# GpSimd folds the sums over the embedding axis a second time: quarters on top of halves, before VectorE's reduction

## The reference

```python
e = jnp.stack([tbl_0[ids[:, 0]], tbl_1[ids[:, 1]],
...
tbl_31[ids[:, 31]]], axis=1)          # (1024, 32, 16)
x0 = e
xk = x0
outs = []
for W in (W0, W1, W2):                # (32, 32, 64), (32, 64, 64), (32, 64, 64)
    xk = jax.nn.relu(jnp.einsum('bmd,bhd,mhk->bkd', x0, xk, W))
    outs.append(jnp.sum(xk, axis=2))  # the sums over d
h = jnp.concatenate([jnp.concatenate(outs, axis=1), dense_ctx], axis=1)
h = jnp.maximum(h @ W_top1 + b_top1, 0.0)
h = jnp.maximum(h @ W_top2 + b_top2, 0.0)
y = h @ W_top3
```

## Time and profile before

| what | value |
|---|---|
| median of 3 runs | 665.38 us (665.16 to 666.02) |
| the profiled execution's own time | 664.73 us |
| its span, first to last instruction | 662.1 us |
| outside the span | 2.63 us |
| mean granted TensorE clock | 0.982 |
| busy: PE, DVE, ACT, POOL | 579.3, 596.7, 357.2, 449.3 us |

### The profile page before, as it was taken

The page is one execution under the profiler, slowest core; times in us unless marked ns, Lnnn a source line. Parts: engine busy times, 40 slices in busy tenths (PEclk is TensorE's granted clock), DMA queues, the critical chain, the costliest instruction groups (busy, mean ns, idle before and its releaser), DMA issues.

```text
span 662.1 us, 7662 instructions
## 1 busy us (share of the span) xinstructions
PE 579.3 (88%) x2868; PEld 206.9 (31%) x2868; DVE 596.7 (90%) x332; ACT 357.2 (54%) x582; POOL 449.3 (68%) x363
## 2 busy tenths in 40 slices
PE   0046779989898989999999989999999989899996
PEld 0012223323232323333334323333334323334355
DVE  1039888999999999999999999999999999999991
ACT  0006463757546564757666465647576664644642
POOL 6676768697958878796969688787969691801010
PEclk9997979999899999999999999999999999999998
DMA  5386594728082744637280837446381908100000
GB/s 157 54 302 170 198 299 103 290 47 304 4 265 90 203 152 109 244 62 290 40 313 3 228 126 208 148 117 236 62 290 34 318 5 286 60 1 0 1 2 0
DMA packets 26990, 96.36 MB, mean 146 GB/s; under 512 B 7397, under 2 KB 12394, under 8 KB 22730
## 3 DMA queue, kind: packets, MB, share of 16 engines
q1 hardware_dynamic: 18762, 93.77, 43.0%
q0 software_dynamic: 8192, 2.11, 2.9%
HBM read 80.12 MB, written 15.73 MB: 145 GB/s over the span
## 4 chain that ended last, share of the span: by engine, by line
DVE 58%; PE 19%; issue 13%; DMA 5%; POOL 2%; ACT 1%; SPq 1%; DVEq 0%; ACTq 0%
DVE prod L415 55%; PE acca L488 6%; PE accb L488 6%; DMA rows<-field_dram 3%; PE acc L464 3%; POOL emb L326 2%; PE spread L536 1%; DVE zb_yv L419 1%; DVE za L419 1%; DMA field_dram<-zin_field 1%; PE acc L507 1%; PE accb L507 1%; SPq L256 1%; ACT zin_field L583 0%; DVE prod L400 0%
## 5 line engine op out<-in xcount | busy, mean ns | idle before, releaser
L326 POOL DMA_INDIRECT emb<-in_table,idx x256 | 246.2, 962 | 82.2 <-issue 71.6
L488 PE MATMUL accb<-prod,w 128*64 128x512 f32 x960 | 223.2, 610 | 28.4 <-DVE prod L415 28.3
L488 PE MATMUL acca<-prod,w 128*64 128x512 f32 x1024 | 231.5, 600 | 7.3 <-DVE prod L415 6.1
L339 POOL TENSOR_TENSOR prod<-rows,mates 128x1024 f32<-128x1024 f32 x70 | 163.8, 2378 | 0.8 <-issue 0.6
L415 DVE TENSOR_TENSOR prod<-rows,x1a 128x2048 f32<-128x2048 f32 x64 | 145.3, 2272 | 5.9 <-ACT x1a L588 3.8
L415 DVE TENSOR_TENSOR prod<-rows,x2b 128x2048 f32<-128x2048 f32 x64 | 145.3, 2271 | 2.1 <-PE accb L488 1.9
L415 DVE TENSOR_TENSOR prod<-rows,x2a 128x2048 f32<-128x2048 f32 x64 | 145.2, 2271 | 1.1 <-PE accb L488 1.1
L415 DVE TENSOR_TENSOR prod<-rows,x1b 128x2048 f32<-128x2048 f32 x64 | 145.2, 2270 | 0.9 <-PE accb L488 0.6
L488 PEld LDWEIGHTS accb<-prod,w 128*64 128x64 f32 x960 | 66.5, 140 | 176.1 <-issue 116.6
L488 PEld LDWEIGHTS acca<-prod,w 128*64 128x64 f32 x1024 | 73.0, 138 | 150.4 <-issue 143.3
L588 ACT ACTIVATE x1a<-acc 64x512 f32<-64x512 f32 x62 | 35.3, 570 | 126.8 <-PE acc L464 126.1
(11 more groups left out here) (56 smaller groups left out, 254.4 us busy)
## 6 DMA issues: line engine op xcount, KB each, us to landing
rows<-field_dram SPq DMA_DIRECT2D x30, 2048.0 KB, 8.9
field_dram<-zin_field SPq DMA_DIRECT2D x32, 256.0 KB
mates<-field_dram SPq DMA_DIRECT2D x16, 512.0 KB, 3.9
emb<-in_table,idx POOLq DMA_INDIRECT x256
field_dram<-zin_field SPq DMA_DIRECT2D x32, 128.0 KB
field_dram<-zin_field SPq DMA_DIRECT2D x16, 192.0 KB
rows<-field_dram SPq DMA_DIRECT2D x2, 1024.0 KB, 7.1
rows<-field_dram SPq DMA_DIRECT2D x1, 1536.0 KB, 12.7
```

The lines of the kernel that those rows point to most:

```text
L326: pool.indirect_dma_start(out=emb[q % EMBS][:, j * EMB:(j + 1) * EMB], out_offset=None, in_=table, in_offset=bass.IndirectOffsetOnAxis(ap= ...
L339: nc.gpsimd.tensor_tensor(prod0[:, (q * L0 + k) % RING0, :], rows[:, slot(q, t), :], mates[:, :], ALU.mult).then_inc(s_prod0p, 1)
L488: mm = nc.tensor.matmul(acc[j % 2][side * HID:(side + 1) * HID, :], (w1 if layer == 1 else w2)[:, step, :], prod[:, (made(layer, s, half, ...
```

## The change

GpSimd adds once more after its half add: values 4 to 7 of each group onto values 0 to 3, in place. The second add reads what the first has written, so GpSimd waits for its own first add through the new semaphore `s_eight`. VectorE's reductions read four values of each group in place of eight; the one that read 16 stays.

```diff
-        s_half12, s_half3 = sem("s_half12"), sem("s_half3")
+        s_eight, s_half12, s_half3 = sem("s_eight"), sem("s_half12"), sem("s_half3")
...
-            def add_halves(z, done):
+            def add_halves(z, n, done):
                 by_d = z.rearrange("k (b d) -> k b d", d=EMB)
-                nc.gpsimd.tensor_tensor(by_d[:, :, 0:DH], by_d[:, :, 0:DH], by_d[:, :, DH:EMB], ALU.add).then_inc(done, 1)
+                nc.gpsimd.tensor_tensor(by_d[:, :, 0:DH], by_d[:, :, 0:DH], by_d[:, :, DH:EMB], ALU.add).then_inc(s_eight, 1)
+                pool.wait_ge(s_eight, n)
+                nc.gpsimd.tensor_tensor(by_d[:, :, 0:QUAD], by_d[:, :, 0:QUAD], by_d[:, :, QUAD:DH], ALU.add).then_inc(done, 1)
...
-                add_halves(zin12[p % 2][:, :], s_half12)
+                add_halves(zin12[p % 2][:, :], max(2 * p, 1), s_half12)
                 if p >= 1:
                     pool.wait_ge(s_z3, 2 * p)
-                    add_halves(zin3, s_half3)
+                    add_halves(zin3, 2 * p + 1, s_half3)
...
-                sum_d(za[:, p * BT:(p + 1) * BT], zin12[p % 2], DH, s_za)
+                sum_d(za[:, p * BT:(p + 1) * BT], zin12[p % 2], QUAD, s_za)
...
-                sum_d(zb[0:HID, p * BT:(p + 1) * BT], zin3, DH if p < LAST else EMB, s_zb)
+                sum_d(zb[0:HID, p * BT:(p + 1) * BT], zin3, QUAD if p < LAST else EMB, s_zb)
```

## The result

The changed kernel takes 656.52 us (median of 4 runs, 655.80 to 657.73) beside 665.52 for the kernel before. The ratio on record is 0.9881, with a 95% interval of 0.9858 to 0.9905; it is not the ratio of these two medians, which is 0.9865, and by it the gain is 7.9 us (6.3 to 9.5). Ratios leave out the executions that count as slow (over 1.5% above the kernel's fastest), medians hold them all. The profiled execution took 656.93 us, with a span of 654.9.

A forecast was written before the change was run, and what follows sets the result against it. VectorE was taken to set the pace in ordinary periods. Shorter sums save 7.0 us, TensorE takes back 1.1, GpSimd's adds cost nothing: 665.4 - 5.9 = 659.5 us, range 657.8 to 662.8.

The forecast's parts named there:

- the bound and the sums: Main loop: VectorE sets the pace in ordinary periods; 26 shortened sums on its path save 0.27 us each, 7.0 us.
- The 5.9: Whole kernel: net gain in us, 7.0 from VectorE's shorter sums less 1.1 taken back by TensorE.
- what TensorE gives back: Two periods where TensorE is full: VectorE arrives 0.54 us earlier and waits 0.54 longer, taking back 1.1 us.
- long-stage periods: Periods from 350.31 and 495.90 us with the tower's longest stage on TensorE: VectorE's stall grows from 0.19 to 0.73 us.
- TensorE's gapless run: From 578.90 us to its last contraction at 650.4, TensorE never waits; this run keeps its 71.5 us.
- A fold: GpSimd's quarter add plus the wait before it: 0.95 us more each, between 0.67 and 1.5.
- GpSimd's wait for its own result: Before each quarter add: 0.24 us, taken from GpSimd's wait for its own memset at the start.
- the foreseen tie: Per period after the change: GpSimd's own work of 35.85 us against a period of 35.81.
- The rule on the shared port: GpSimd and VectorE share an SBUF read port, so shifted work might gain nothing; the prediction set this term at 0.
- the 2.27 named: Sign of being wrong: VectorE's products taking more than 2.27 us beside the quarter adds.
- the rival on TensorE's clock: Slow pair at 173.07 after a 1.93 us wait: clock fall goes, 1.2 us less, 658.3 us; chance 0.13.
- another pattern of the clock: Sign of being wrong: the profile after shows TensorE's granted clock in another pattern; no size given.

The follow-up runs named there:

- third fold on both: Changed kernel plus a third GpSimd add (values 2 and 3 onto 0 and 1) for zin12 and zin3, VectorE summing two values: 659.77 us, ratio 0.9941.
- reader's half: Changed kernel without GpSimd's quarter adds: VectorE's reductions read four values, values 4 to 7 left out: 655.32 us, ratio 0.9860.
- before again: The kernel before the change, run once more unchanged: 664.34 us, ratio 1.0001.
- quarters only: Kernel before plus GpSimd's quarter adds, VectorE still reducing eight values: 664.13 us, ratio 1.0004.
- filled gap: Kernel before plus three unread matmuls in TensorE's 1.93 us wait in steps 3, 5, 7 and 9: 660.23 us, ratio 0.9937.
- later sum: Kernel before with the sum of zin3 one unit later, all other work the same: 660.49 us, ratio 0.9958.
- zin12 alone: Kernel before with the change made for zin12 only, zin3 keeping one half add and a sum of eight: 658.34 us, ratio 0.9902.
- both third folds: Changed kernel plus a third GpSimd add, in one run for zin12 and zin3 (659.77 us), in the other for zin12 only (653.96 us).

## Why the prediction missed

**Right: the bound and the sums.** VectorE set the pace, and the path counted held. From 131 us to the last sum of `zin12` the profile before takes 510.5 us and the one after 503.3; less the one fall of 1.2, the difference is 6.0 us, forecast 5.9. A sum moves the next product by 0.33 us as forecast. The 5.9 was earned, not luck: its parts came out one by one.

**Right: what TensorE gives back.** The stall in the long-stage periods is 0.74 us, start to start (forecast 0.73), and TensorE's gapless run is 71.5 us after too (572.00 to 643.50). The long-stage periods are 36.56 us. The prediction's list for the profile after put them near 36.35, but its own sum, 0.54 won and 0.54 given back, leaves them at 36.55.

**Right in kind, off in size: GpSimd.** A fold costs 0.82 us, not 0.95. The term that was too large is GpSimd's wait for its own result: 0.24 us after a memset at the start, 0.08 us after a half add. So the foreseen tie was a room of 0.31 us. The removed and the added half, each alone, show that the adds cost nothing in the main loop. That the room is nearly nothing was right: a third fold on both tips it.

**The rule on the shared port.** Had the rule of the Trainium skill applied that the prediction names (page "Perfetto Trace Analysis", section Optimizing Scalar/DVE Operations: GpSimd and VectorE share an SBUF read port), quarter adds would have slowed VectorE. With them alone its products keep 2.20 us from start to start, and the ratio is 1.0004 (0.9990 to 1.0018). One sign of being wrong seems to have come: products are shown as 2.28 us long after, over the 2.27 named. It is not the quarter adds: the median is 2.275 us with the reader's half alone, which has none, and 2.269 in the third trace of the changed kernel, which has them, and the starts stay 2.20 us apart in all.

**Wrong: the clock.** The failed step is the rival on TensorE's clock. It took the one fall that the profiled execution showed for all that there were, priced its going at 1.2 us and gave it 0.13, though it said in the same place that the change shortens the wait. So the bottom of the range, 657.8, stood for one fall gone. Three traces with the wait at 1.92 us (before, before again, quarters only) show 1, 3 and 4 falls out of 4. Nine traces with the wait at 1.66 us or less, all without late rows (changed kernel three times, reader's half, filled gap, later sum, zin12 alone, both third folds), show none in 36. Shortening the wait alone in the kernel before brings 4.2 us (2.7 to 5.6) by the fill and 2.8 us (0.8 to 4.8) by the later sum; counted, the 8 falls of three traces are 2.7 an execution, 3.2 us. With the 6.0 of the path that makes 8.8 to 10.2 us, and by their ratios the three comparisons of the changed kernel say 7.9, 7.8 and 8.9 us. The two agree within the intervals, no closer.

Two more places vary by about 1.5 us from execution to execution. At the end TensorE's last large tower piece takes 3.44, 3.21 and 3.50 us in the three traces of the changed kernel. It takes 3.66, 2.05 and 2.05 in the three with the sums of the kernel before (before, before again, quarters only), and 2.05 with the reader's half alone; the granted clock of the stretch around it is 0.92 in the profile after. If that is more than chance, it takes some of the gain back. At the start a double pair of TensorE, near 95 us and behind a wait of 2.46 us, takes 8.6 to 8.8 us in eight of the twelve traces, of both kernels, and about 7.1 in the others. Whether the change has a part in either was not tried.

The misread sign was there. Four waits of 1.9 us stood in the profile before, the one with the fall and these three:

```profile
136.72 3.65 PE L488 MATMUL accb<-prod,w 128*64 128x512 f32 x16 [1.92 <-DVE prod L415]
...
210.62 3.65 PE L488 MATMUL accb<-prod,w 128*64 128x512 f32 x16 [1.91 <-DVE prod L415]
...
246.97 3.65 PE L488 MATMUL accb<-prod,w 128*64 128x512 f32 x16 [1.93 <-DVE prod L415]
```

The same wait stood there four times and the effect once, in a single execution. That asked for a price between one fall and four, 1.2 to 4.8 us, and for a range that reaches down to 654.7 (659.5 - 4.8). The last of the prediction's signs of being wrong, another pattern of the clock, came true.

## What to carry to other kernels

Where an engine saves time before another's wait, look at what the shorter wait does to that engine's clock: here removing the falls alone was worth 2.8 and 4.2 us beside 6.0 of saved work, and could be had without the change, by moving one instruction or filling the wait. When a profile shows one rare event behind a condition that repeats, price all the repetitions, since one execution is one draw. And count a helper engine's room as drift over the whole stretch, not per period: a helper that needed 0.4 us a period more than there was cost about 0.5 us over eleven periods, and one that needed 1.0 more made the kernel some 4 us slower than the change.

## What the runs showed of the hardware

TensorE's clock fell after waits of 1.92 us in 8 of 12 cases and after none of 36 waits of 0.43 to 1.66 us, with the same work around them; each fall made a pair take 5.35 us in place of 3.65 and the period 1.20 us longer. In the eight traces of the slower jobs it fell after 34 of 53 waits of 1.9 to 4.3 us and after no shorter one. The number of falls differed between executions of the same kernel, 1 and 3. A second add on GpSimd that waits for the first started 0.08 us after its end, and 31 added GpSimd adds of 0.72 us changed neither VectorE's pace of 2.20 us a product nor the time (ratio 1.0004). In some jobs VectorE waited 3.8 us every second period, in part for transfers of field rows by the profile, and the kernel took 690 us in place of 664, with one chip seen at both.
